# Self-attention on one Trainium2 core: five elementwise steps of each row moved from VectorE to GpSimd

## The reference

```python
x = x + attention(layernorm(x))          # 32 heads of 16, 8 key/value heads, rotary, causal
x = x + cross_attention(layernorm(x), ctx)   # 32 heads of 128, 8 key/value heads
x = x + layernorm(x) @ dequantised(w).T + bias
```

## Time and profile before

| What | Before |
|---|---|
| Median of 3 runs | 992.04 us (990.35 to 992.8) |
| Profiled execution: span from first to last instruction | 989.3 us |
| TensorE busy | 927.3 us (94%) |
| VectorE busy | 742.3 us (75%) |
| ScalarE busy | 604.4 us (61%) |
| GpSimd busy | 568.9 us (58%) |
| Self-attention (to its last `xT_lo` on VectorE) | 0 to 218.9 us of the span |

### The profile page before, as it was taken

One profiled execution on the slowest core, in us unless ns is written; L12 is line 12 of the kernel. 1 busy time (PEld: TensorE's weight loads), 2 busy tenths in 40 slices (PEclk: granted clock), 3 DMA queues, 4 the chain that ended last, 5 costly groups with the idle time before them and its releaser, 6 DMA issues.

```text
span 989.3 us, 17511 instructions
## 1 busy us (share of the span) xinstructions
PE 927.3 (94%) x5484; PEld 797.2 (81%) x5492; DVE 742.3 (75%) x1555; ACT 604.4 (61%) x2226; POOL 568.9 (58%) x593
## 2 busy tenths in 40 slices
PE   5689999769999999999999999999999999999977
PEld 5567777548888888888888888888888888888765
DVE  6678988855877777777777777777777777789964
ACT  1568888615856676665667556765756675575530
POOL 6522322224865685677458656856774686468643
PEclk8799999779999999999999999999999999999999
DMA  5000020006666566557645665665576456654431
GB/s 203 12 12 13 12 87 12 1 1 223 211 219 205 168 209 208 172 167 231 211 149 186 213 210 169 198 209 178 167 236 196 150 175 209 214 170 150 134 117 54
DMA packets 101148, 149.84 MB, mean 151 GB/s; under 512 B 11840, under 2 KB 77376, under 8 KB 98880
## 3 DMA queue, kind: packets, MB, share of 16 engines
q1 hardware_dynamic: 101056, 148.71, 47.2%
HBM read 87.85 MB, written 60.82 MB: 150 GB/s over the span
## 4 chain that ended last, share of the span: by engine, by line
PE 69%; DVE 4%; ACT 1%; POOL 1%; issue 1%; DMA 1%; SPq 0%; DVEq 0%; POOLq 0%
PE ps_kv L73 17%; PE ps_y L73 17%; PE ps_q L73 17%; PE ps_o L73 8%; PE ps_s L73 8%; ACT ps_s L1090 1%; DVE p L1202 1%; PE ps_f L73 1%; DVE neg_max L1190 1%; POOL pT_raw L1008 1%; DVE p_blocks L1206 0%; DVE raw_wkv L1269 0%; DMA out<-raw_wq 0%; DVE kT_lo L1229 0%; DVE f_stats L1259 0%
## 5 line engine op out<-in xcount | busy, mean ns | idle before, releaser
L1090 ACT ACTIVATE ps_s<-ps_s,bias,q_rms 128x256 f32<-128x256 f32 x256 | 136.8, 535 | 139.5 <-DVE bias L1194 139.5
L1001 POOL TENSOR_TENSOR qT_lo<-qk_raw,qT_hi 128x512 fp32r<-128x512 f32 x64 | 84.6, 1322 | 202.6 <-ACT qT_hi L1119 202.6
L1008 POOL TENSOR_TENSOR pT_raw<-pT_raw,pT_hi_sb 128x1024 fp32r<-128x1024 f32 x64 | 154.1, 2408 | 11.9 <-ACT pT_hi_sb L1113 11.6
L1107 ACT ACTIVATE q_squares<-ps_q 128x128 bf16<-128x128 f32 x256 | 67.5, 278 | 112.0 <-DVE qk_blocks L1224 112.0
L73 PE MATMUL ps_y<-wo_hi,oT_hi 128*128 128x512 f32 x256 | 101.7, 397 | 4.9 <-DVE oT_lo L1240 4.9
L73 PE MATMUL ps_q<-wq_lo,xT_hi 128*128 128x512 f32 x256 | 101.4, 396 | 0.0
L73 PE MATMUL ps_q<-wq_hi,xT_lo 128*128 128x512 f32 x256 | 101.1, 395 | 0.0
L73 PE MATMUL ps_y<-wo_lo,oT_hi 128*128 128x512 f32 x256 | 101.1, 395 | 0.0
L1206 DVE STREAM_TRANSPOSE p_blocks<-p 128x512 f32<-128x512 f32 x128 | 91.1, 711 | 13.3
L73 PE MATMUL ps_y<-wo_hi,oT_lo 128*128 128x512 f32 x256 | 101.0, 394 | 0.0
L73 PE MATMUL ps_q<-wq_hi,xT_hi 128*128 128x512 f32 x256 | 100.9, 394 | 0.0
(11 more groups left out here) (217 smaller groups left out, 2940.2 us busy)
## 6 DMA issues: line engine op xcount, KB each, us to landing
p_scratch<-p_blocks SPq DMA_DIRECT2D x64, 512.0 KB, 3.0
pT_raw<-p_scratch SPq DMA_DIRECT2D x256, 128.0 KB, 3.1
qk_scratch<-qk_blocks SPq DMA_DIRECT2D x64, 384.0 KB, 3.5
qk_raw<-qk_scratch SPq DMA_DIRECT2D x256, 96.0 KB, 2.9
raw_wq<-in_x_wq SPq DMA_DIRECT2D x8, 1024.0 KB, 7.8
raw_wo<-in_x_wo SPq DMA_DIRECT2D x8, 1024.0 KB, 7.5
raw_wkv<-in_x_wkv SPq DMA_DIRECT2D x8, 512.0 KB, 5.0
ctx_raw<-in_ctxT SPq DMA_DIRECT2D x8, 256.0 KB, 2.7
```

What stands on the lines that cost most here:

```text
L1001: pool.tensor_tensor(qT[1][:].rearrange("p g (i c) -> p g i c", i=4), qk_raw[s % 2][:, :, 0:XG, :].rearrange("p i g c -> p g i c"), f32(qT ...
L1008: pool.tensor_tensor(raw, f32(raw), f32(pT_hi_sb[:].rearrange("p i t x -> p (i t x)")), ALU.subtract).then_inc(pT_lo, 1)
L1090: e = act.activation(scores, scores, ACT.Exp, bias=bias[:, g:g + 1], scale=q_rms[:, s % 4, g:g + 1], accum_out=total[:, g:g + 1])
L1107: i = act.activation(q_squares[:, g, :], ps_q[:, g * XD:(g + 1) * XD], ACT.Square, scale=XD ** -0.5, accum_out=q_mean[:, g:g + 1])
```

## The change

Four steps leave VectorE's queue for GpSimd's: `queries_low`, `normalised_2`, `output_low` and, for rows 2 to 7, `normalised` (rows 0 and 1 stay). From `inverse_totals` the spread becomes GpSimd's `inverse_wide`; the reciprocal stays. `rstd_2` and `normalised_2` are one function now. GpSimd's loop is written anew, `context(n)` stands later in it, and TensorE waits for the low parts of the cross-attention's weights in two steps.

```diff
+            def normalised(m):
+                pool.wait_ge(rstd_ok, 2)
+                wait(pool, xnT_ps, m)
+                pool.tensor_scalar(xn[:], acc[:, m, :], moments[:, m, 0:1], rstd[:, m:m + 1],
+                                   ALU.subtract, ALU.mult).then_inc(xn_ok, 1)
-            def rstd_2(n):
+            def normalised_2(n):
...
+                pool.wait_ge(rstd2_ok, n + 1)
+                wait(pool, x2T_ps, n)
+                pool.tensor_scalar(xn2[:], acc[:, n, :], moments2[:, 0:1], rstd2[:, 0:1],
+                                   ALU.subtract, ALU.mult).then_inc(xn2_ok, 1)
+            def inverse_wide(n):
+                pool.wait_ge(inv_ok, n + 1)
+                wait(pool, invT_ps, n)
+                pool.tensor_copy(inv_wide[:], inv[:].rearrange("p (j x) -> p x j", x=G).unsqueeze(3)
+                                 .broadcast_to([P, G, KVH, HD])).then_inc(wide_ok, 1)
...
-            for m in range(1, B + 2):
-                if m < B:
-                    rotate_keys(m)
-                if m <= B:
-                    context(m - 1)
-                if m < B:
-                    rotate_queries(m)
+            for n in range(B + 1):
+                if n + 1 < B:
+                    rotate_keys(n + 1)
+                    rotate_queries(n + 1)
+                if n + 2 < B:
+                    normalised(n + 2)
+                if n + 1 < B:
+                    queries_low(n + 1)
...
-                if m >= B:
-                    cross_weights_low(m - B)
-                if m >= 2:
-                    rstd_2(m - 2)
+                if n >= 1:
+                    normalised_2(n - 1)
+                if n < B:
+                    context(n)
+                if n == B - 1:
+                    cross_weights_low(0)
+                if n < B:
+                    inverse_wide(n)
+                    output_low(n)
+                if n == B - 1:
+                    cross_weights_low(1)
...
             def inverse_totals(n):
                 dve.wait_ge(exp_done, UNITS * (n + 1))
+                wait(dve, wide_ok, n)
                 dve.reciprocal(inv[:], total[:]).then_inc(inv_ok, 1)
-                dve.wait_ge(inv_ok, n + 1)
-                wait(dve, invT_ps, n)
-                dve.tensor_copy(inv_wide[:], inv[:].rearrange("p (j x) -> p x j", x=G).unsqueeze(3)
-                                .broadcast_to([P, G, KVH, HD])).then_inc(wide_ok, 1)
...
-            pe.wait_ge(xw_lo, 2)
+            pe.wait_ge(xw_lo, 1)
...
             project_output(B - 1)
+            pe.wait_ge(xw_lo, 2)
             split_matmuls(pe, mem["ps_q"][:], [(xT[0][:, c, 0:S], xT[1][:, c, 0:S], wq[0][:, c, :], wq[1][:, c, :])
```

More of the change, by code:

```diff
@@ L244, in rotate_keys, with queries_low @@
                 pool.tensor_tensor(k_stack[:, :, :, 1, :], keys, f32(k_stack[:, :, :, 0, :]), ALU.subtract).then_inc(k_lo, 1)
-            def rstd_2(n):
+            def queries_low(m):
+                pool.wait_ge(q_hi, m + 1)
+                pool.tensor_tensor(q_stack[:, :, 2:4, :], rot[:, 0:H, :].unsqueeze(2).broadcast_to([P, H, 2, HD]),
+                                   f32(q_stack[:, :, 0:2, :]), ALU.subtract).then_inc(q_lo, 1)
+            def normalised(m):
[4 more added lines that the diff above has]
+            def normalised_2(n):
                 pool.wait_ge(moments2_ok, n + 1)
@@ L251, in rstd_2, with output_low @@
                 pool.tensor_tensor(rstd2[:], rstd2[:], minus_half[:, 0:1], ALU.pow).then_inc(rstd2_ok, 1)
+                pool.wait_ge(rstd2_ok, n + 1)
[7 more added lines that the diff above has]
+                                 .broadcast_to([P, G, KVH, HD])).then_inc(wide_ok, 1)
+            def output_low(n):
+                pool.wait_ge(o_hi, n + 1)
+                pool.tensor_tensor(oT[1][:], o[:], f32(oT[0][:]), ALU.subtract).then_inc(o_lo, 1)
             def context(n):
@@ L267, in _ @@
             rotate_keys(0)
+            queries_low(0)
             pool.wait_ge(moments_ok, 2)
@@ L272, in _ @@
             pool.tensor_tensor(rstd[:, 2:B], rstd[:, 2:B], minus_half[:, 2:B], ALU.pow).then_inc(rstd_ok, 1)
-            for m in range(1, B + 2):
-                if m < B:
-                    rotate_keys(m)
-                if m <= B:
-                    context(m - 1)
-                if m < B:
-                    rotate_queries(m)
-                if m == 1:
+            for n in range(B + 1):
[6 more added lines that the diff above has]
+                    queries_low(n + 1)
+                if n == 0:
                     pool.wait_ge(wo_in, 16)
@@ L419, in pad_values @@
                 i.then_inc(v_ok, 1)
[L421 to L424, removed]
             def key_tiles(m):
@@ L454, in output @@
                 dve.tensor_tensor(o[:], ps_o[:].rearrange("p (g s) -> p g s", g=G), invT[:], ALU.mult).then_inc(o_ok, 1)
-            def output_low(n):
-                dve.wait_ge(o_hi, n + 1)
-                dve.tensor_tensor(oT[1][:], o[:], f32(oT[0][:]), ALU.subtract).then_inc(o_lo, 1)
             def residual(n):
@@ L465, in statistics_2 @@
                 dve.wait_ge(acc_ok, n + 1)
+                wait(dve, xn2_ok, n)
                 dve.bn_stats(stats2[:], acc[:, n, :]).then_inc(stats2_ok, 1)
@@ L468, in statistics_2 @@
                 dve.bn_aggr(moments2[:], stats2[:]).then_inc(moments2_ok, 1)
[L470 to L473, removed]
             def x2_low(n):
@@ L523, in _ @@
                     probs_transposed(n, 1)
-                if later and n >= 0:
-                    normalised(n + 2)
                 if n >= 1:
@@ L529, in _ @@
                     maxima(n, 4)
-                if after:
-                    queries_low(n + 1)
                 if now:
@@ L544, in _ @@
                     probs_transposed(n, 4)
-                if n >= 1:
-                    normalised_2(n - 1)
                 if n == B - 2:
@@ L565, in _ @@
                     pad_values(n + 2)
-                if now:
-                    output_low(n)
                 if after:
```

## The result

The changed kernel takes 1015.14 us (median of 4 runs, 1013.52 to 1017.25), the kernel before on the same chip 991.26 us (990.35 to 992.8): a ratio of 1.0242, with a 95% interval of 1.0213 to 1.0271. It is slower by 24 us; the forecast was 994.6 us, the range ended at 1004. The profiled execution took 1017.25 us, its span is 1015.5 us, 26.2 us above that of before.

What follows compares the result with a forecast made beforehand. TensorE's own queue plus a 3.4 us hand-over was taken to set the 20 us row. Terms 7.0 - 1.0 - 2.5 - 1.2 + 0.3 = +2.6 on the 989.3 us span, plus 2.7 us, gave 994.6 us; range 990.0 to 1004.0.

Steps and rivals of the forecast that it cites:

- What GpSimd must do in a middle row: Middle rows: normalising and spreading priced at 0.61 us each, giving GpSimd 5.5 us more, 11.4 of 20.
- `normalised` ... Cost 0: Middle rows: GpSimd has normalised by 108.2, before the queries' low part, so no time is lost.
- only 0.2 us to spare: Middle rows: GpSimd's `queries_low` ends at 111.1 and TensorE wants it at 111.31, cost 0.
- `normalised_2` ... Cost 0 in itself: Middle rows: normalising ends at 117.6; lateness would only move TensorE's wait from the spread to the transposes before it.
- the wait for the spread: Rows 1 to 5: `inverse_wide` behind the context makes TensorE wait 1.4 us per row, +7.0 us together.
- Rival 3: Rows 1 to 5: a second gap drops the clock in every row, 3.2 us each, +16, 1011 us; chance 0.05.
- Ahead of row 0 and in row 0: Start of the self-attention: earlier `queries_low` on GpSimd gains, -1.0 us ahead of row 0 and -2.5 in it.
- Rows 6, 7 and the end: Last rows: shorter wait for the spread in row 6, -1.2 us; row 7 and the end together +0.3.
- the gap of 1.20 us: Middle rows: TensorE's wait for `xn_low` before the second query tiles stays, so relieving VectorE gains nothing.
- `queries_low` and `output_low` cost nothing there: Middle rows: GpSimd delivers both low parts before TensorE wants them, cost 0 each.
- GpSimd's normalisation or spread far from 0.61 us: Sign of being wrong: GpSimd's instruction times for these two steps differ much from the assumed price.
- a granted clock below 1.00 between 65 and 165 us: Sign of being wrong: the clock falls below the 2.4 GHz level in that stretch.

Runs made afterwards that it cites:

- e9: Changed kernel with GpSimd's two normalisations as one multiplication by the inverse deviation, mean not subtracted; 1004.58 us in a single run.
- e4: Changed kernel with GpSimd's two normalisations using constants 0 and 1 in place of mean and inverse deviation; 1013.15 us, ratio 1.0233.
- e1: Changed kernel with both normalisations of rows 2 and later back on VectorE, context still ahead of the spread; 990.07 us, ratio 0.9985.
- e2: Changed kernel with the context moved behind the spread on GpSimd, normalisations staying on GpSimd; 994.49 us, ratio 1.0047.
- e5: Changed kernel with only GpSimd's order edited: context and the normalisation of `xn`, one row earlier, behind the spread; 992.52 us, ratio 1.0015.
- e6: Kernel before with only the two normalisations moved to GpSimd; 995.34 us, ratio 1.0046.
- e7: Kernel before with only the queries' low parts moved to GpSimd; 984.69 us, ratio 0.9930.
- e8: Kernel before with only spread and output's low part moved to GpSimd, context behind the spread, cross weights waited for as changed; 985.66 us, ratio 0.9949.
- e3: Changed kernel with both normalisations back on VectorE and the context behind the spread on GpSimd; 976.47 us, ratio 0.9876.

## Why the prediction was wrong

- **The step that failed** is the price in "What GpSimd must do in a middle row": "the lower bound is the cast, 0.61 us, the upper the subtraction with two, 1.29 us. I take 0.61". The normalisation took 2.08 us, outside both bounds; the spread took 0.61 as taken. The bounds were drawn by counting full operands, and the runs show that the form and its arithmetic steps count too (1.57 and 1.93 us in e9 and e4). The Trainium skill (GPSIMD Engine Reference, section 4.1 Engine selection) calls one-input work roughly line rate; the spread is near that (0.61 us, 0.43 on VectorE), the normalisation is not: 2.08 us against 0.54 us on VectorE.
- "`normalised` ... Cost 0" fell with it. The "only 0.2 us to spare" were those of `queries_low`, which still makes nobody wait in the middle rows; the wait of 0.66 us came ahead of the transposes of `xn`, a place that the text does not time. "`normalised_2` ... Cost 0 in itself" became 1.03 us; there the text had seen that lateness would show as a wait ahead of the transposes of `xn2`.
- **The mechanism was right.** With 2.08 in place of 0.61, the forecast's own steps give the row that was measured. GpSimd's `xn` at 108.2 becomes 109.7, 0.8 us behind TensorE, which took it up here in the kernel before:

```profile
108.83 0.60 PE L583 MATMUL a_ps_t<-ident,a_xn 128*128 128x128 f32 x4
```

The chain to the spread becomes 1.4 + 1.47 = 2.87 us late; measured, TensorE needs 6.36 us from its mark to the spread's transposes (123.56 to 129.92) and needed 3.49 (115.29 to 118.78), 2.87 more. Together that is 3.7 us, and the row grew by 3.70. In the middle rows at full clock the term that was mis-sized is the price alone, 1.47 us too low for each of two steps. That the wait for the spread was forecast at 1.4 us and is 1.45 in each of rows 1 to 5 is luck: TensorE waits out part of the chain just before, ahead of `xn2`, and with the normalisations back (e1) a row is only 0.78 us longer than before.

- Rival 3, the half clock, had a chance of 0.05 and stood at nothing in the sum. It came in part: in three of five middle rows, some 1.5, 2.7 and 1.6 us. In e4 and e9, with waits of 2.8 and 2.2 us for GpSimd in a row, spells came too, in four and three of the rows; in e1, e2, e5 and e6, with 0.6 to 1.7 us, none did. That spells go with the longer waits is what these profiles show; no run varied the clock alone.
- **The ends.** Ahead of row 0 and in row 0 -3.5 us was forecast, -1.35 came: GpSimd normalises row 2's `xn` (43.91 to 46.00) ahead of the queries' low part, which so started at 45.97 and not at 44.5, the same price again. The first wait for `q_stack` did shrink, to 1.55 us. Rows 6, 7 and the end were forecast at -0.9 and lost 1.6: the normalisation took 2.60 us in row 6 and 3.13 in row 7, and TensorE waited 1.32 and 0.70 us there in row 6 (2.93 before) and, with the context and a weight's subtraction of 2.35 us in the chain, 1.65 and 3.65 us in row 7 (4.64 before).
- **The sum.** Of the 23.6 us between +2.6 forecast and +26.2 in the span, the price makes 11.4 in rows 1 to 5, the spells 5.8, the ends 4.7; 1.8 lie behind the self-attention.
- Right were: the gap of 1.20 us stays in every row, so VectorE's relief gives the middle rows nothing (17.77 to 11.98 us busy, row longer); `queries_low` and `output_low` cost nothing there (e7, e8); the moved pieces gain at the ends (e3, e7, e8).
- Two of the signs that the forecast named for being wrong came: "GpSimd's normalisation or spread far from 0.61 us" and "a granted clock below 1.00 between 65 and 165 us".

## What to carry to other kernels

An instruction's price on another engine need not follow its operand count: here it went by the form of the instruction; where the trace has no row of that form, the range must reach well above the nearest row, since one late step in a chain is paid in every row. An idle engine is no free place: what counts is how long each chain through it is, from its last input to the instruction that waits, so put work without a deadline (here the context) behind the steps that are waited for. Of five steps moved together three gained 12 us (e3), and the two normalisations, added to these with the context behind the spread, cost 17 (e2); alone they cost 4.6 (e6). Such costs do not simply add up: move and time the steps apart and together.

## What the runs showed of the hardware

- GpSimd, 128x512 fp32: copy or cast 0.61 us, subtraction of two tiles 1.29, multiplication by one scalar per partition 1.57, subtraction and multiplication 1.93 with constants and 2.08 with scalars per partition.
- In these rows it depends on GpSimd's operation which engine gives way, though VectorE's started second each time. VectorE's copy of the spread took 2.41 us beside GpSimd's subtraction and 0.43 alone; in rows 1 to 5 of e6 it took 0.43 to 0.62 us inside GpSimd's normalisation, which kept its 2.09. Beside VectorE's casts of weights it was the normalisation that grew, from 2.09 to 2.60 and 3.13 us, and the casts took 0.70 and 1.23 us, without a hold-up. Row 7 of the changed kernel:

```profile
218.71 3.13 POOL L265 TENSOR_SCALAR a_xn<-x,a_moments,a_rstd 128x512 f32<-128x512 f32 x1
```

```profile
218.73 1.23 DVE L502 CAST wq_hi<-raw_wq 128x2048 fp32r<-128x2048 f32 x1
```

The Trainium skill (SBUF — State Buffer, section SBUF: two separate sides) has the later of the two blocked for the whole of the other's instruction; the spread in e6 started 0.44 us behind the normalisation and ended 1.05 us ahead of it, so for this pair the measurement differs.
